# Weight quantisation of a fused attention + FFN block: issued in one block ahead of attention instead of between its steps

## The reference

```
h = layernorm(x) * (1 + ca) + sa
x = x + ga * attention(h)          # 16 heads of 64; keys are h itself, queries h @ w_att_val
h = layernorm(x) * (1 + cb) + sb
x = x + gb * ffn(h)                # w_gate, w_up: 4096x1024, w_down: 1024x4096
def _weight_quant(w):
    scale = 1.0 / clip(mean(abs(w)), 1e-05)
    return clip(round(w * scale), -1, 1) / scale
```

## Time and profile before

| | |
|---|---|
| time, median of 3 runs (lowest to highest) | 8024.12 us (8014.3 to 8024.84) |
| profiled execution: time / span of its slowest core | 8024.84 / 8023.3 us |
| spans of the 8 cores | 7956.5 to 8023.3 us |
| mean granted TensorE clock, slowest core | 0.758 |
| busy: PE / DVE / ACT / POOL | 4352.5 / 3114.6 / 2334.5 / 161.7 us |
| end of the value stage, start of quantisation set-up | 1450 us |
| attention, first score matmul to last block's normalisation | 1461 to 4892 us |
| FFN | 5413 us to the end |

### The profile page before, as it was taken

The page is one execution under the profiler, slowest core; times in us unless marked ns, Lnnn a source line. Parts: engine busy times, 40 slices in busy tenths (PEclk is TensorE's granted clock), DMA queues, the critical chain, the costliest instruction groups (busy, mean ns, idle before and its releaser), DMA issues.

```text
span 8023.3 us, 61607 instructions; the slowest of 8 cores (7956.5 to 8023.3 us)
## 1 busy us (share of the span) xinstructions
PE 4352.5 (54%) x19208; PEld 1610.2 (20%) x19208; DVE 3114.6 (39%) x2821; ACT 2334.5 (29%) x2268; POOL 161.7 (2%) x307
## 2 busy tenths in 40 slices
PE   5342259277765778478848884444333343343433
PEld 1110024122221223122313221221111111111111
DVE  1536533166654655255525553442011120111211
ACT  0010100066754667367737762000000000000000
POOL 0200000000000000000000000000000000000000
PEclk8665579688887889688969887777666676676766
DMA  4822123222221210100010001213223223232232
GB/s 147 286 79 88 69 82 100 69 70 82 68 84 54 70 36 3 39 4 20 3 39 4 3 5 44 63 43 94 82 75 98 74 84 93 69 101 76 81 97 66
DMA packets 369792, 550.77 MB, mean 69 GB/s; under 512 B 43202, under 2 KB 307010, under 8 KB 360260
## 3 DMA queue, kind: packets, MB, share of 16 engines
q1 hardware_dynamic: 304996, 353.58, 14.8%
q0 software_dynamic: 35808, 125.86, 4.9%
q10 hardware_dynamic: 28672, 67.39, 2.3%
HBM read 454.11 MB, written 92.54 MB: 68 GB/s over the span
## 4 chain that ended last, share of the span: by engine, by line
DMA 36%; PE 23%; DVE 17%; ACT 17%; issue 6%; SPq 1%; ACTq 1%; DVEq 0%; POOL 0%; POOLq 0%
DMA wus<-d_wuq 14%; ACT p L783 9%; DMA wds<-d_wdq 9%; ACT phi L788 7%; DMA vg<-d_v 6%; PE vps L666 4%; PE o_psA L768 3%; PE o_psB L768 3%; DVE sumr L813 2%; PE o_ps L914 2%; PE s_ps L753 2%; DVE plo L792 1%; PE rb_ps L815 1%; DMA wgs<-d_wgq 1%; PE dn_ps L1134 1%
## 5 line engine op out<-in xcount | busy, mean ns | idle before, releaser
L792 DVE TENSOR_TENSOR plo<-p,phi 128x1024 bf16<-128x1024 f32 x1024 | 1248.2, 1225 | 1348.6 <-ACT phi L788 1338.5
L783 ACT ACTIVATE p<-s_ps,negCp 128x1024 f32<-128x1024 f32 x1024 | 1134.3, 1108 | 1175.1 <-DVE oglo L828 667.8
L788 ACT ACTIVATE phi<-p 128x1024 bf16<-128x1024 f32 x1024 | 1081.9, 1057 | 96.6 <-ACT p L783 3.4
L768 PE MATMUL o_psA<-phi,vg 128*65 128x512 bf16 x2048 | 814.7, 398 | 510.1 <-DMA vg<-d_v 427.5
L1052 PE MATMUL g_ps<-wgs,kq2T 128*128 128x512 bf16 x1024 | 473.8, 463 | 848.2 <-DMA wus<-d_wuq 754.8
L753 PE MATMUL s_ps<-qg,kg 64*128 64x512 bf16 x6144 | 879.0, 394 | 32.9 <-DVE qtot L355 16.8
L768 PE MATMUL o_psB<-phi,vg 128*65 128x512 bf16 x2048 | 791.1, 386 | 0.0
L1062 ACT ACTIVATE sil<-g_ps,gsc 128x512 f32<-128x512 f32 x128 | 87.9, 687 | 2329.3 <-PE u_ps L1055 2329.2
L1134 PE MATMUL dn_ps<-wds,kq3T 128*128 128x512 bf16 x1024 | 342.3, 510 | 523.5 <-DMA wds<-d_wdq 523.5
L1066 DVE TENSOR_SCALAR upv<-u_ps,usc 128x512 f32<-128x512 f32 x128 | 96.1, 751 | 1188.5 <-PE u_ps L1055 1188.5
L1055 PE MATMUL u_ps<-wus,kq2T 128*128 128x512 bf16 x1024 | 468.1, 457 | 0.0
(11 more groups left out here) (179 smaller groups left out, 3284.2 us busy)
## 6 DMA issues: line engine op xcount, KB each, us to landing
wgs<-d_wgq SPq DMA_DIRECT2D x512, 128.0 KB, 2.4
wus<-d_wuq SPq DMA_DIRECT2D x512, 128.0 KB, 2.5
wds<-d_wdq SPq DMA_DIRECT2D x512, 128.0 KB, 2.1
qwb<-wgT POOLq DMA_DIRECT2D x64, 512.0 KB, 5.5
qwb<-wuT POOLq DMA_DIRECT2D x64, 512.0 KB, 5.4
qwb<-wdT POOLq DMA_DIRECT2D x64, 512.0 KB, 4.7
wm<-wmod SPq DMA_DIRECT2D x16, 1536.0 KB, 7.4
d_v<-vaug ACTq DMA_DIRECT2D x64, 260.0 KB, 2.2
```

Source lines behind the costliest of these rows:

```text
L768: last = e.matmul(ops_[:], vg[lp][:, hcol:hcol + 65], rt[:, hh * 512:(hh + 1) * 512], start=(pi == 0 and kc == 0), stop=(pi == 2 and kc == ...
L783: sc(lambda e, par=par, pp4=pp4: e.activation(p32[pp4][:], s_ps[par][:], AF.Exp, bias=negCp[:, pair:pair + 1], scale=0.125), [f"sS{par}", ...
L788: sc(lambda e, pp4=pp4: e.activation(phi[pp4][:], p32[pp4][:], AF.Copy), [f"p32_{pp4}", f"phi{pp4}"], [f"phi{pp4}"], tag=f"phic{pair}_{thq ...
L792: dve(lambda e, pp4=pp4: e.tensor_tensor(plo[pp4][:], p32[pp4][:], phi[pp4][:], op=AL.subtract), [f"p32_{pp4}", f"phi{pp4}", f"plo{pp4}"], ...
```

## The change

The tasks are issued in one go, behind the three `quant_stageBC` calls and ahead of attention's first operation, and the call inside the loop is taken away. The call behind attention (L856) stays, with an empty list.

```
         for (d_w, d_wqt, nchunks, width, j, wqname) in QSPECS:
             quant_stageBC(d_w, d_wqt, nchunks, width, j, wqname)
+        drain_qc(10 ** 9)
 
         with contextlib.ExitStack() as p4:
...
                             emit_av(*flat[j], j)
-                            if j % 4 == 3:
-                                drain_qc(1)
                             if flat[j][1] == KC - 1:
```

## The result

The changed kernel is slower, by the ratio 1.0691 (95% interval 1.0677 to 1.0705) over runs on the same chips. The profiled execution took 8569.38 us, on a span of 8567.8 us; the prediction was 8587 us.

What follows compares the result with a forecast made beforehand. No single limit; ACT works only in attention, and the block becomes a serial load-store loop. First value matmul 659.8 us later, less 97.6 given back, is 562 on 8024.8: 8587 us, range 8530 to 8690.

Steps and rivals of the forecast that it cites:

- The serial loop: Block ahead of attention: each load waits behind the previous task's store; 8.3, 7.9, 7.4 us per task, 758 us in all.
- fixed 3.39 us per task: Block: everything in a task's loop except the landing, namely issues, releases, `qpos` and `qwq`.
- The landings: Block's task loads, issue to landed: 4.9 us gate, 4.5 up, 4.0 down, 428.8 us over 96 tasks.
- rule on the landing: Block's 512 KB loads by the skill page's fit: 3.2 us each, 307 us together, 8465 us total; prediction preferred the trace.
- No attention work under the block, the `vg` wait as its cover: Attention's start: three steps, then PE and ACT idle; `vg` loads hidden; first value matmul 659.8 us later, at 2249.1.
- What attention gives back: Pairs 0 to 2 without tasks run like pairs 4 and 5: 97.6 us gained, 1.02 us per task.
- Nothing behind attention absorbs it: Behind attention's fence: projection and FFN unchanged, so the whole 562 us delay reaches the end.
- A: Block's loads get faster, landing in 3.8 us: 64 us less, 8523 us; chance 6%.
- B: Block's loads get slower, one microsecond more per load giving 8683 us; chance 9% for more than half a microsecond.
- B's far end: All block loads land in stage A's 8.4 us: 377 us more, 8964 us; no separate chance given.
- C: Block's loads run ahead from four buffers: about 4.5 us per task, 432 us block, 8265 us; chance 1%.
- D: Block as short as DVE's work, about 196 us, matched by attention's gain: about 8024 us, not slower; chance 2%.

Runs made afterwards that it cites:

- the two kernels with the `vg` edit: Each `vg` piece named separately, its two parts loaded consecutively: against the kernel before, ratio 0.9527, 7603.24 us; against the changed kernel, 8246.4 us, single run.

## Why the prediction was right

Point by point, by its steps:

- *The serial loop.* Right. The fixed 3.39 us per task stands: from 1722.71 to 1730.96 is 8.25 us, of which 5.03 us lie between the load at 1723.25 and `qpos` at 1728.28. Taking the load out of the loop, and then a part of the wait for the store, brought the task to 4.6 and 3.69 us, so POOL's order and the one `qwq`, not DVE or the memory, made its length.
- *The landings.* A little too long: 4.9, 4.5 and 4.0 us were taken, 4.5, 4.3 and 4.0 measured, 19 us less over the 96. Some 10 us of that came back, since medians leave out the slow loads beside the `vg` loads. From the first load to the first value matmul it was predicted 759.8 us and measured 2246.85 - 1495.73 = 751.1 us on core 0, and 740 to 754 us on the eight cores. The prediction's rule on the landing, 3.2 us a load and 8465 us in all, did not come: the smallest of core 0's 96 landings took 3.7 us.
- *No attention work under the block, the `vg` wait as its cover.* Right; the cover was put at 100 us and is 95 by the two kernels with the `vg` edit, and the block behind attention, which lacks it, costs 90 us more. The `vg` issues took 176 us beside the block instead of 132; they were through long before its end.
- *What attention gives back.* Predicted 97.6 us from pairs 4 and 5 of the kernel before: pair 0 340.3, pair 1 363.9, pair 2 464.8. Measured 340.6, 361.7 and 463.9, and 99.8 us in the kernel with the block behind. The size is right, its reading only in part: today it is not so that nobody waits for the loads. 26.8 of the 97.6 us are DVE's waits for a load at the ends of the three pairs, so that by estimate DVE's work as such cost attention some 0.74 us per task, (97.6 - 26.8) / 96. (Attention's last slice in the earlier trace rows is 24, not 23.)
- *Nothing behind attention absorbs it.* Right to the FFN's start, 549.8 us later by the medians; 562 had been predicted. On the slowest cores it is 553.7 us (5989.1 on core 0 against 5435.4 on core 2), 8 us less than predicted. The other 9 of the 18 us between 8587 and 8569.38 are in the FFN (2587.9 us on the slowest core before, 2578.7 on the slowest after), which the prediction took to be unchanged; how the FFN falls on the slowest core is chance as far as the runs show.
- *Rivals.* A (3.8 us landings) and B (8.4) lie on either side of what came; B's far end took the slowest of the three in stage A, where gate landed in 6.5 us and down in 5.3. C's 8265 us is near what the kernel with loads ahead shows, 8235.81, when POOL's order is changed. D never came near: the break-even of 2.04 us per task was missed even with all four buffers and two `qwq` in use, at 3.69.

That the medians of 4.0 to 4.9 us would hold was the uncertain part, and the range was right to be drawn around it. Gate's loads landed 0.4 us faster than in attention; in the block their median was 4.8 us beside the `vg` loads and 4.1 behind them. Why they take 4.9 us in attention was not tested.

## What to carry to other kernels

Before moving background work out of a loop, measure its latency and not its engine time: here 2.03 us of DVE per task were 7.8 us in a block, while attention had paid 1.0 us for a task between its steps. Look in the issuing engine's own order for a load behind a store of the same stream; buffers do not help while the queue has that order, and the time from a load's issue to the turn of its user must exceed its landing wherever the work is put. And check first whether the wait that the eye falls on is the costly one: a shared name that made each group's 64 loads serial was worth 412 us here, the tasks at most 98.

## What was not expected of the hardware

- **The FFN's length differs between cores on the same work.** From its first matmul to the span's end it takes 2528.2 us on core 1 and 2587.9 us on core 2 in the kernel before, at the same granted clock (0.70 and 0.69), and over the runs here 2503 to 2597 us. Three quarters of its chain on core 2 are DMA landings (`wus` 43.2%, `wds` 28.5%, `wgs` 4.2%). Two rows, the kernel before and the one with the block behind, core 2, matmuls of `g_ps`, first and last start (some records of the second are missing from its trace):

```profile
L1052 PE MATMUL g_ps<-wgs,kq2T x1024: 376/379/634, 5435.4 to 7858.3; 128*128 128x512 bf16 x171
```

```profile
L1051 PE MATMUL g_ps<-wgs,kq2T x983: 376/379/634, 6071.3 to 8438.7; 128*128 128x512 bf16 x197
```

  2422.9 against 2367.4 us. What sets it wasn't found. It differs by 60 us between the cores of one run, as much as some of the effects above, which is why they are told by the FFN's start.
- **A 512 KB landing was nearly independent of the rate up to 179 GB/s** (medians of 4.0 to 4.9 us at a mean of 70, 105 and 179 GB/s, with one load in flight or several) and grows at 224 GB/s (4.7 to 5.0) and in stage A at 279 GB/s, where it is 5.3 us for down, 6.5 for gate and 8.4 for up. The short `vg` loads are hit earlier: 1.8 us in the wait before, 2.2 beside the block, 3.3 beside the block with loads ahead.
- **POOL pauses 2.5 us behind a store at two places of the 96 tasks**, behind the first and once more in the up pieces, in the kernel before, in the changed one and with the block behind attention alike. Its cause is open.
